# Attention scores from four row tiles of 32 rows, one per head, with the queries used in place

## The reference

```python
q = (hs @ wq.T)...   # 32 heads of 64
k = (hs @ wk.T)...   # 8 heads of 64, each used by 4 query heads
v = (hs @ wv.T)...
q = x * cos + rotate_half(x) * sin   # rope, k too
scores = einsum('bhqd,bhkd->bhqk', q, k) / sqrt(64), masked above the diagonal
probs = softmax(scores)
o = einsum('bhqk,bhkd->bhqd', probs, v)
return o @ wo.T
```

## Time and profile before

| | us |
|---|---|
| median of 3 runs | 856.08 |
| the runs | 851.24 to 856.58 |
| the profiled execution | 854.13 |
| its span, first instruction to last | 852.2 |
| TensorE busy | 753.5 (88%) |
| VectorE busy | 493.2 (58%) |
| ScalarE busy | 481.4 (56%) |
| GpSimd busy | 460.3 (54%) |

### The profile page before, as it was taken

One profiled execution on the slowest core, in us unless ns is written; L12 is line 12 of the kernel. 1 busy time (PEld: TensorE's weight loads), 2 busy tenths in 40 slices (PEclk: granted clock), 3 DMA queues, 4 the chain that ended last, 5 costly groups with the idle time before them and its releaser, 6 DMA issues. The chain is left out here.

```text
span 852.2 us, 18997 instructions
## 1 busy us (share of the span) xinstructions
PE 753.5 (88%) x5895; PEld 637.9 (75%) x5895; DVE 493.2 (58%) x1943; ACT 481.4 (56%) x1537; POOL 460.3 (54%) x690
## 2 busy tenths in 40 slices
PE   3699999999999999999999999826039999999994
PEld 2578888888888888888888888622027888888883
DVE  5797666666666667667567667384942333333331
ACT  1568777777777777777777777625212222222221
POOL 1456656556566565565565666346633545444452
PEclk9899999999999999999999999968559999999998
DMA  5434122122121221221221212058631223333230
GB/s 191 133 112 106 36 60 65 37 63 62 40 64 51 50 63 46 56 60 42 63 54 48 63 40 63 14 169 253 202 137 26 47 45 53 52 54 52 45 50 2
DMA packets 51905, 61.16 MB, mean 72 GB/s; under 512 B 10368, under 2 KB 45440, under 8 KB 51552
## 3 DMA queue, kind: packets, MB, share of 16 engines
q1 hardware_dynamic: 40144, 48.48, 20.0%
q0 software_dynamic: 7488, 9.36, 6.8%
q10 hardware_dynamic: 4176, 2.11, 0.9%
HBM read 26.34 MB, written 9.32 MB: 42 GB/s over the span
## 5 line engine op out<-in xcount | busy, mean ns | idle before, releaser
L818 POOL TENSOR_SCALAR probs<-exps,inv_sums 128x128 f32<-128x128 f32 x256 | 97.0, 379 | 195.7 <-DVE inv_sums L676 135.3
L557 ACT COPY pT<-probsT 128x384 f32<-128x384 f32 x256 | 122.0, 477 | 80.4 <-PE probsT L434 80.4
L434 PE MATMUL probsT<-tables,probs 128*128 128x128 f32 x768 | 129.8, 278 | 5.4 <-ACT pT L557 4.0
L550 ACT ACTIVATE exps<-masked,neg_max 128x256 f32<-128x256 f32 x256 | 127.5, 498 | 0.0
L819 POOL TENSOR_SCALAR probs<-exps,inv_sums 128x256 f32<-128x256 f32 x256 | 124.4, 486 | 0.0
L548 ACT ACTIVATE exps<-masked,neg_max 128x128 f32<-128x128 f32 x256 | 103.2, 403 | 37.0 <-DVE neg_max L670 36.8
L1411 POOL DMA_INDIRECT out<-y,to_token x39 | 61.9, 1587 | 102.4 <-DVE y L1380 78.2
L421 PE MATMUL scores<-kT,qT 64*128 64x128 f32 (+1 forms) x1024 | 103.3, 342 | 5.1 <-DMA qT<-rotated 5.1
L670 DVE CUSTOM_DVE_ANT_0 masked<-scores,tables 128x256 f32<-128x256 f32 x256 | 107.5, 420 | 0.0
L668 DVE CUSTOM_DVE_ANT_0 masked<-scores,tables 128x128 f32<-128x128 f32 x256 | 72.1, 282 | 54.2 <-PE scores L421 32.4
L434 PEld LDWEIGHTS probsT<-tables,probs 128*128 128x128 f32 x768 | 87.2, 141 | 19.5 <-issue 9.7
(11 more groups left out here) (156 smaller groups left out, 1876.4 us busy)
## 6 DMA issues: line engine op xcount, KB each, us to landing
qT<-rotated SPq DMA_DIRECT2D x256, 64.0 KB, 2.2
kT<-k_cos SPq DMA_DIRECT2D x64, 128.0 KB, 3.4
experts_w_out<-w_in SPq DMA_DIRECT2D x16, 512.0 KB, 4.6
raw<-w_attn SPq DMA_DIRECT2D x20, 256.0 KB, 3.3
experts_w_out<-w_out SPq DMA_DIRECT2D x2, 2048.0 KB, 9.7
out<-x_all SPq DMA_DIRECT2D x8, 256.0 KB, 2.3
xn_rows<-experts_w_out ACTq DMA_DIRECT2D x4, 512.0 KB, 4.5
x_all<-x SPq DMA_DIRECT2D x1, 1792.0 KB, 10.6
```

The costliest lines, as they stand in the source:

```text
L434: mm = nc.tensor.transpose(p_bank[:, at:at + P], probs[:, h, at:at + P], ident)
L550: nc.scalar.activation(exps[:, h, P:3 * P], masked[:, h, P:3 * P], ACT.Exp, bias=neg_max[:, h, 1:2], scale=-1.0, accum_out=sums[:, h, 1:2] ...
L557: nc.scalar.copy(pT[:, n % 2, h, :], p_bank[:, 0:3 * P]).then_inc(pT_done, 1)
L818: nc.gpsimd.tensor_scalar(probs[:, h, 0:P], exps[:, h, 0:P], inv_sums[:, h, 0:1], 1.0, ALU.mult, ALU.mult)
```

## The change

The weights of the queries are laid out such that a projected row is 32 h + i, not 4 i + h: each head's 32 channels of a half lie together, in one of four groups of rows. The queries are then used from `rotated` where they are, and `qT`, `move_q` and its semaphores go. The sine and cosine tables exist in two orders, one for the queries and one for the keys, so that the table has 1920 columns instead of 1152. The keys are copied to four groups of rows, with both halves of the channels: four copies of 256 KB instead of 128 KB. Each head's scores are two products of 32 rows, one for each half, that add up in the bank. All four heads' products of one tile and half stand next to each other. The semaphore for the scores is raised once, by 4, behind the last product; before the first product the scores wait for all four evictions of the turn before. `rotate_q` waits for the scores that read its buffer, where it waited for the copies.

```diff
-ATTN_TABLE = 3 * SEQ + 3 * P
+ATTN_TABLE = 6 * SEQ + 3 * P
...
-    attn = np.concatenate([cosT, -sinT, sinT, mask, ident], 1)
+    attn = np.concatenate([cos_q, -sin_q, sin_q, cos_k, -sin_k, sin_k, mask, ident], 1)
...
-    qT = sb("qT", [P, 2, PAIRS, SEQ])
-    kT = sb("kT", [P, 2, HALF, SEQ])
+    kT = sb("kT", [P, 2, HALF, 2, SEQ])
...
-        def move_q(m, s, first=False):
-
-            sp.wait_ge(q_rotated, m + 1)
-            if not first:
-
-                sp.wait_ge(s_ps, (m - 1) * GROUP)
-            for odd in range(2):
-                for a in range(2):
-                    at = odd * HD + a * 32
-                    sp.dma_start(qT[at:at + 32, s, :, :], rotated[odd:P:2, s, a, :]).then_inc(q_in[s], 16)
-
         def move_k(b, half):
...
-            for a in range(2):
-                for copy in range(2):
-                    at = copy * HD + a * 32
-                    sp.dma_start(kT[at:at + 32, half, :, :], k_cos[:, a, :]).then_inc(k_in[half], 16)
+            for h in range(GROUP):
+                sp.dma_start(kT[h * 32:h * 32 + 32, half, :, :, :], k_cos[:, :, :]).then_inc(k_in[half], 16)
...
-            pe.wait_ge(q_in[g % 2], (n // 2 + 1) * 64)
+            pe.wait_ge(q_rotated, n + 1)
             if g % HALF == 0:
                 pe.wait_ge(k_in[g // HALF], b * 64 + 64)
-            for pair in range(PAIRS):
-                if n > 0:
-
-                    pe.wait_ge(s_read, (n - 1) * GROUP + 2 * pair + 2)
-                for tt in range(TT):
-                    for odd in range(2):
-                        rows = slice(odd * HD, odd * HD + HD)
-                        mm = nc.tensor.matmul(s_bank[2 * pair + odd][:, tt * SEQ:tt * SEQ + (tt + 1) * P],
-                                              qT[rows, g % 2, pair, tt * P:(tt + 1) * P],
-                                              kT[rows, g // HALF, g % HALF, 0:(tt + 1) * P], start=True, stop=True)
-                mm.then_inc(s_ps, 2)
+            if n > 0:
+
+                pe.wait_ge(s_read, n * GROUP)
+            for tt in range(TT):
+                for a in range(2):
+                    for h in range(GROUP):
+                        rows = slice(h * 32, h * 32 + 32)
+                        mm = nc.tensor.matmul(s_bank[h][:, tt * SEQ:tt * SEQ + (tt + 1) * P],
+                                              rotated[rows, n % 2, a, tt * P:(tt + 1) * P],
+                                              kT[rows, g // HALF, g % HALF, a, 0:(tt + 1) * P],
+                                              start=(a == 0), stop=(a == 1))
+            mm.then_inc(s_ps, GROUP)
...
             pool.wait_ge(q_parts, m + 1)
             if not first:
-                pool.wait_ge(q_in[m % 2], m // 2 * 64)
+                pool.wait_ge(s_ps, (m - 1) * GROUP)
```

More of the change, by code:

```diff
@@ L79, in shape_constants @@
     cos, sin = np.cos(ang).astype(np.float32), np.sin(ang).astype(np.float32)
-    cosT, sinT = np.repeat(cos.T, GROUP, 0), np.repeat(sin.T, GROUP, 0)
+    cos_q, sin_q = np.tile(cos.T, (GROUP, 1)), np.tile(sin.T, (GROUP, 1))
+    cos_k, sin_k = np.repeat(cos.T, HALF, 0), np.repeat(sin.T, HALF, 0)
     q, k = np.arange(P)[:, None], np.arange(P)[None, :]
@@ L109, in attention @@
     tables = sb("tables", [P, ATTN_TABLE])
-    cos = tables[:, 0:SEQ].rearrange("p (o t) -> p o t", o=1).to_broadcast([P, 2, SEQ])
-    sin = tables[:, SEQ:3 * SEQ].rearrange("p (a t) -> p a t", a=2)
-    mask = tables[:, 3 * SEQ:3 * SEQ + 2 * P]
-    ident = tables[:, 3 * SEQ + 2 * P:3 * SEQ + 3 * P]
+    cos_q = tables[:, 0:SEQ].rearrange("p (o t) -> p o t", o=1).to_broadcast([P, 2, SEQ])
+    sin_q = tables[:, SEQ:3 * SEQ].rearrange("p (a t) -> p a t", a=2)
+    cos_k = tables[:, 3 * SEQ:4 * SEQ].rearrange("p (o t) -> p o t", o=1).to_broadcast([P, 2, SEQ])
+    sin_k = tables[:, 4 * SEQ:6 * SEQ].rearrange("p (a t) -> p a t", a=2)
+    mask = tables[:, 6 * SEQ:6 * SEQ + 2 * P]
+    ident = tables[:, 6 * SEQ + 2 * P:6 * SEQ + 3 * P]
     raw = sb("raw", [P, SLOTS, PIECE_COLS])
@@ L174, in attention @@
     v_done = sem("v_done")
-    q_in = [sem("q_in0"), sem("q_in1")]
     k_in = [sem("k_in0"), sem("k_in1")]
@@ L289, in _ @@
         load_piece(SLOTS + 1)
-        move_q(0, 0, True)
-        move_q(1, 1, True)
         for i in range(SLOTS + 2, SLOTS + EARLY):
@@ L295, in _ @@
         for s in range(2):
-            sp.wait_ge(q_in[s], 64 * (TURNS // 2))
             sp.wait_ge(k_in[s], 64 * BATCH)
@@ L645, in rope_q @@
             halves = x_bank[:, :].rearrange("p (a t) -> p a t", a=2)
-            nc.vector.tensor_tensor(by_cos[:, :, :], halves, cos, ALU.mult)
-            nc.vector.tensor_tensor(by_sin[:, :, :], halves[:, ::-1, :], sin, ALU.mult).then_inc(q_parts, 1)
+            nc.vector.tensor_tensor(by_cos[:, :, :], halves, cos_q, ALU.mult)
+            nc.vector.tensor_tensor(by_sin[:, :, :], halves[:, ::-1, :], sin_q, ALU.mult).then_inc(q_parts, 1)
         def rope_k(b, half):
@@ L656, in rope_k @@
             halves = x_bank[:, :].rearrange("p (a t) -> p a t", a=2)
-            nc.vector.tensor_tensor(k_cos[:, :, :], halves, cos, ALU.mult)
-            nc.vector.tensor_tensor(k_sin[:, :, :], halves[:, ::-1, :], sin, ALU.mult).then_inc(k_parts, 1)
+            nc.vector.tensor_tensor(k_cos[:, :, :], halves, cos_k, ALU.mult)
+            nc.vector.tensor_tensor(k_sin[:, :, :], halves[:, ::-1, :], sin_k, ALU.mult).then_inc(k_parts, 1)
         def maxima(b, g, h):
@@ L939, in _ @@
         sp.dma_start(consts[:, :], t["route_consts"]).then_inc(consts_in, 16)
-        sp.dma_start(ident[:, :], t["attn_consts"][:, 3 * SEQ + 2 * P:]).then_inc(consts_in, 16)
+        sp.dma_start(ident[:, :], t["attn_consts"][:, 6 * SEQ + 2 * P:]).then_inc(consts_in, 16)
         sp.dma_start(gate[:, :, :], t["gate"].rearrange("p (k e) -> p k e", k=KT)).then_inc(consts_in, 16)
@@ L1251, in _ @@
     def _(sp):
-        sp.dma_start(ident[:, :], t["attn_consts"][:, 3 * SEQ + 2 * P:]).then_inc(ident_in, 16)
+        sp.dma_start(ident[:, :], t["attn_consts"][:, 6 * SEQ + 2 * P:]).then_inc(ident_in, 16)
         for p in range(RING):
@@ L1455, in laid_out @@
 def laid_out(x, wq, wk, wv, wo, gate, w0, w1, w2):
-    wqT = wq.T.reshape(KT, P, KV_HEADS, GROUP, 2, HD // 2).transpose(1, 2, 0, 4, 5, 3).reshape(P, KV_HEADS, PIECE_COLS)
+    wqT = wq.T.reshape(KT, P, KV_HEADS, GROUP, 2, HD // 2).transpose(1, 2, 0, 4, 3, 5).reshape(P, KV_HEADS, PIECE_COLS)
     wkT = wk.T.reshape(KT, P, 2, HALF, 2, HD // 2).transpose(1, 2, 0, 4, 5, 3).reshape(P, 2, PIECE_COLS)
```

2 lines of the change are left out of this document (removed).

## The result

The changed kernel takes 874.12 us (median of 4 runs, 873.34 to 875.33) where the kernel before took 855.63 beside it (851.24 to 856.58). The ratio is 1.0228, with a 95% interval from 1.0190 to 1.0265: slower by 18.5 us. The forecast was 864.5, slower by 10: right in sign, inside the range of 850 to 878, and too small by nearly half. 874.12 is at the very top of the forecast's own 857 to 874. The profiled execution of the changed kernel took 873.34 us, span 871.5; that is the one compared with 854.13 and 852.2 here.

A forecast was written before the change was run, and what follows sets the result against it. The prediction took TensorE, busy 88% of the span, as the bound. Its terms, 1.0 + 5.6 + 1.6 + 0.6 + 2.0 - 0.8 = +10.0 us on the profiled 854.13, gave 864.1, set to 864.5; range 850 to 878.

The forecast's parts named there:

- The late signal: Scores signalled only after all four heads' last product: VectorE's first eviction moves from 1.16 to 1.81 us after group start.
- The products: TensorE's score groups: again 1.30 us of steps, third and fourth heads starting slightly later, 16 ns a turn, +1.0 us.
- Rivals A and B: Score group: A, only two heads at a time, 947 us, chance 0.09; B, packing or supply loss, 892 us, chance 0.05.
- Turns with the rope of keys: Turns g=2 and g=5: the query projection waits for VectorE's late k_sin, 13 x 0.43 us, +5.6 us.
- Short turns: 16 turns without rope of keys, batches 1 to 7: scores wait for the previous fourth eviction, 0.1 each, +1.6 us.
- The last turns: Two last turns, without rope: transposes wait for ScalarE's copy behind the cast, +0.3 us each, +0.6 us.
- Batch 0: First batch, VectorE also splitting weights: waits for evictions and ropes, 0.5 us for four turns, +2.0 us, between 1 and 3.5.
- The start: First scores: no wait for query copies gains up to 2.6 us, against bigger key copies and table; net -0.8 us.

The follow-up runs named there:

- b_late_both: The kernel before with one score signal after all four heads and the wait for all four earlier evictions ahead of the group: 868.77 us, ratio 1.0176.
- b_late_signal: The kernel before with the four heads' scores signalled once, after the last of sixteen products; waits for evictions stay per pair: 866.94 us, ratio 1.0134.
- a_stag: The changed kernel with batch 0's first key copies issued head by head behind weight pieces, each turn's scores awaiting their own head: 869.87 us, ratio 1.0168.
- a_pairs: The changed kernel with heads 0 and 1 wholly first, then heads 2 and 3, each pair signalled when done: 892.32 us, ratio 1.0422.
- a_short: The changed kernel with head 1's transposes ahead of the value products and ScalarE's copy ahead of the first exponentials, in turns without another projection: 871.34 us.
- a_ksplit2: The changed kernel with the first key copies split by head, the first head's four issued first, then twelve for the others: 873.66 us, ratio 1.0207.

## Why the forecast was right in sign and too small

Two steps failed: the path by which the short turns grow (a mechanism that I had wrong) and the start (the price of the key copies, and with it the sign). The late signal itself, the largest term, was right. Term by term:

- **The products, +1.0.** Right mechanism. The group takes 1.52 in place of 1.51; between b_late_both and the changed kernel batches 1 to 7 differ by 454.69 - 453.06 = 1.6 us, 0.03 a turn, where I took 0.016; 0.3 of it is the wait for the keys in batch 7, which I had at 0, since I took 5.4 + 3 us from issue to landing where the copies take 10.2. So 1.3 us, or 0.02 a turn, is left. Rivals A and B, 0.14 of the chance, are refuted. What I had against A, four products overlapping in the earlier trace rows, was the right sign to read.
- **Turns with the rope of keys, +5.6.** Right, and shown three times over: by the wait, by the one edit in the kernel before, and by moving the rope. Measured 13 x 0.50 = 6.5. The eviction came 0.68 later, not 0.65. From k_sin's end to the projection 0.06 us passed (321.45 to 321.51), the signal's 0.05 that I had assumed, so the slack was 0.21 and the wait 0.47.
- **Short turns, +1.6.** This step failed in its mechanism. I had TensorE wait for the fourth eviction, 0.1 each. b_late_both against b_late_signal shows that wait as nothing. The turns waited for ScalarE's copy of head 1 behind the cast: it ended 0.29 us later in the turn (4.34 in place of 4.05), had 0.10 of slack (4.30 less 4.05 less 0.15 from copy to transposes), and so made TensorE wait 0.19 of the 0.23 by which they grew. In batches 1 to 6 that is 12 x 0.23 = 2.8 us. In batch 7 the four short turns grew by 0.22, 0.56, 0.22 and 0.22; 0.3 of the 0.56 (g=3) is the wait for the keys, so 0.9 is left: 3.7 in place of 1.6. I had put the cast's delay of 0.38 down, and carried it only to the inverse and the query rope on VectorE; the copy that stands directly behind the cast on ScalarE, and the transposes that wait for it, I did not follow. I had done so for the last turns alone.
- **The last turns, +0.6.** The last turn but one grew by 7.46 - 7.15 = 0.31; right.
- **Batch 0, +2.0.** b_late_signal and b_late_both end batch 0 at 101.7 and 100.4, 2.4 later than the mean of those with the order of before: about right, with a spread as large. The 0.38 that I had read off for its last turn came as 0.40, with 0.26 and 0.28 at g=4 and g=6: there the wait for the fourth eviction is real.
- **The start, -0.8.** This step failed too, and in sign: 28.2 to 28.6 in place of 26.0 to 26.6, so +2. The mis-sized term is the key copies: I priced their second half MB at 2.7 us by the 197 GB/s of the earlier trace rows. 0.5 MB had taken 5.5 us and 1 MB took 10.2, so it cost 4.7, and the stretches show 127 to 140 GB/s at full share. Besides, -0.8 isn't what my own terms add up to: 2.7 against 2.6, and part of 1.2, is +0.1 to +1.3; I had leaned to a gain for the reason that the bigger copies replace the removed ones, which has no price. The table, which I charged with 1.2 us in part, cost nothing. a_stag, which takes the scores out from behind the copies, gives 4.2 us back, of which the first scores and batch 0 show 2.1.

In sum 6.5 for the ropes, 3.7 for the short turns, 0.3 for the last turn but one and 1.6 for products and keys are 12.1, against the 12.2 measured in batches 1 to 7 (the first terms hold a little of the 1.6 too); for the same parts I had 5.6 + 1.6 + 0.3 + 0.9 = 8.4. Batch 0 with the start is 4.2 where I had 1.2. So 3.8 and 3.0 of the 8.5 us that I was short are placed, and the rest is not. My lower end of 857 is not their sum either: the low bounds as I gave them, with 5.6 for the ropes and 0.6 for the last turns kept, are 859.

## What to carry to other kernels

Splitting these products over four row tiles in place of two left their time and moved their first result: every head has the same share of rows for the whole group, so the first is ready when the last is, 0.68 us later here. Ask for each signal not only how much work stands ahead of it but when the first waiting engine needs it, and follow the delay down every engine's order, to each instruction that stands behind the delayed one. Work that needs none of the late results can be put ahead of the wait: the rope of the keys cost nothing there, and 7.1 us came back, 5.5 of them in the batches that repeat well. And follow a copy that doubles to its every use: here its spare time went from 5 us to 0.3 to 0.6 in batches 1 to 6.

## What the runs showed of the hardware

- Products of other row groups started ahead of earlier ones in the list (a_pairs, above), and two pairs of heads took 2.07 us where strictly one after the other would have been some 2.8, an estimate from the 1.30 us of steps for each pair and 0.2 for the switch.
- Four row tiles of 32 rows at once had steps as long as two of 64 rows: 1.52 us for 32 products (changed kernel) against 1.51 for 16 (kernel before). The Trainium skill's 3.07x for four of them ("TensorE: Matmul & The Clock Gate", Part 3, the table of measured speedups) isn't borne out for this shape; its row is for 512 columns, these products have 128 and 256.
- An issue on SyncE's queue took 0.6 us, whether it moved 64 KB or 256 KB (2.46 us for four in a_ksplit2, 2.61 for four in the changed kernel).
- Key copies of 0.5 MB took 5.5 us from the first issue to the last landing (kernel before) and those of 1 MB 10.2 us (changed kernel).
- Values behind three transposes started 0.45 us after the first of them (a_short), a projection 0.30 (changed kernel).
